# Cross-attention and mixture of experts: the first head's softmax sums on GpSimd, and an opening in another order

## The reference

```python
# cross attention: queries and keys from layernorm(x), further keys from the context
q = (ln @ Wq)                                  # per batch and head: 1024 x 64
kv = concatenate([xn @ Wkv, ln @ Wkv], axis=1)  # 77 context keys and 1024 token keys
qn, kn = rmsnorm(q, qn_g) * scale, rmsnorm(k, kn_g)
attn = softmax(einsum('bhid,bhjd->bhij', qn, kn) + mask)
x = x + einsum('bhij,bhjd->bhid', attn, v) @ Wout + bout
# then a shared expert and the best 2 of 8 experts for each token, on layernorm(x)
x = x + shared(x) + routed(x)
```

## Time and profile before

| | before |
|---|---|
| median of three runs | 2646.66 us |
| the profiled execution | 2644.76 us, span 2643.1 us |
| TensorE busy | 2502.3 us (95%) |
| VectorE busy | 1857.7 us (70%) |
| ScalarE busy | 1691.6 us (64%) |
| GpSimd busy | 1312.2 us (50%) |
| mean granted TensorE clock | 0.978 of full |

### The profile page before, as it was taken

The page is one execution under the profiler, slowest core; times in us unless marked ns, Lnnn a source line. Parts: engine busy times, 40 slices in busy tenths (PEclk is TensorE's granted clock), DMA queues, the critical chain, the costliest instruction groups (busy, mean ns, idle before and its releaser), DMA issues. The chain is left out here.

```text
span 2643.1 us, 45087 instructions
## 1 busy us (share of the span) xinstructions
PE 2502.3 (95%) x14568; PEld 2048.0 (77%) x14568; DVE 1857.7 (70%) x2507; ACT 1691.6 (64%) x2286; POOL 1312.2 (50%) x784
## 2 busy tenths in 40 slices
PE   3699999999999999999999999986989999999998
PEld 3577777777777777777777777754989999999997
DVE  6666776767777777677677767765877557776775
ACT  2477777777777777778778777774332334454453
POOL 4344553555444544454445544541542526666675
PEclk8799999999999999999999999998989999999999
DMA  5665556545664566455655565545741449999996
GB/s 186 193 159 141 155 156 165 152 134 167 165 157 133 161 162 169 131 169 151 163 148 142 162 166 149 137 131 122 169 122 55 141 145 319 321 321 321 325 320 176
DMA packets 256912, 466.62 MB, mean 177 GB/s; under 512 B 65575, under 2 KB 145755, under 8 KB 251848
## 3 DMA queue, kind: packets, MB, share of 16 engines
q1 hardware_dynamic: 230166, 406.54, 54.6%
q0 software_dynamic: 25696, 58.82, 7.9%
q10 hardware_dynamic: 978, 0.34, 0.1%
HBM read 280.90 MB, written 79.85 MB: 136 GB/s over the span
## 5 line engine op out<-in xcount | busy, mean ns | idle before, releaser
L664 DVE TENSOR_TENSOR pr_lo<-pr,pr_hi 128x1024 fp32r<-128x1024 f32 x576 | 818.5, 1429 | 356.1 <-ACT pr_hi L765 350.6
L764 ACT ACTIVATE pr<-ps_s 128x1024 f32<-128x1024 f32 x512 | 525.9, 1027 | 332.9 <-PE ps_s L883 313.5
L765 ACT ACTIVATE pr_hi<-ps_s 128x1024 fp32r<-128x1024 f32 x512 | 522.1, 1020 | 0.0
L897 PE MATMUL ps_o<-pr_hi,vA 128*65 128x512 f32 x1152 | 464.9, 404 | 20.6 <-DVE o_second L603 11.3
L410 POOL TENSOR_TENSOR sq<-raw 128x1024 f32<-128x1024 f32 (+1 forms) x96 | 183.6, 1913 | 584.6 <-ACT raw L719 584.6
L899 PE MATMUL ps_o<-pr_lo,vA 128*65 128x512 f32 x1152 | 455.1, 395 | 0.0
L898 PE MATMUL ps_o<-pr_hi,vC 128*65 128x512 f32 x1152 | 453.2, 393 | 0.0
L1547 ACT ACTIVATE ht<-f_ps_h,b 128x256 f32<-128x256 f32 x440 | 184.6, 470 | 339.7 <-PE f_ps_h L1479 339.6
L414 POOL TENSOR_TENSOR rs<-ss,minus_half 128x16 f32<-128x16 f32 (+1 forms) x96 | 261.0, 2719 | 246.0 <-DVE ss L649 246.0
L883 PE MATMUL ps_s<-qq_hi,kk 128*128 128x512 f32 x1152 | 362.8, 396 | 8.2 <-ACT pr_hi L765 6.6
L883 PE MATMUL ps_s<-qq_lo,kk 128*128 128x512 f32 x1152 | 361.7, 395 | 0.0
(11 more groups left out here) (195 smaller groups left out, 3857.0 us busy)
## 6 DMA issues: line engine op xcount, KB each, us to landing
w<-w1S_dram SPq DMA_DIRECT2D x160, 512.0 KB, 6.0
lnT_sb<-lnT_dram SPq DMA_DIRECT2D x31, 2304.0 KB, 8.5
w2raw<-in_L_ffn_Wproj SPq DMA_DIRECT2D x78, 512.0 KB, 6.9
qq_hi<-q_hi SPq DMA_DIRECT2D x128, 256.0 KB, 4.8
qq_lo<-q_lo SPq DMA_DIRECT2D x128, 256.0 KB, 5.0
kk<-k_hi SPq DMA_DIRECT2D x64, 288.0 KB, 5.1
kk<-k_lo SPq DMA_DIRECT2D x64, 288.0 KB, 5.4
w1S_dram<-cut POOLq DMA_DIRECT2D x36, 512.0 KB, 4.2
```

The costliest lines, as they stand in the source:

```text
L664: v.tensor_tensor(pr_lo[:, d % RING, :], pr[:, d % 2, :], pr_hi[:, d % RING, :].bitcast(F32), ALU.subtract).then_inc(s_lo, 1)
L764: act.activation(pr[:, d % 2, :], ps_s[:, d % 2, :], ACT.Exp, bias=bias)
L765: act.activation(pr_hi[:, d % RING, :], ps_s[:, d % 2, :], ACT.Exp, bias=bias).then_inc(s_exp, 1)
L897: mm(out, upper, pr_hi[:, r, cols], start=k == 0, stop=False)
```

## The change

**The first head (h = 0) of every window**, in the form without maxima:

- `vA` and `vC` become one tile `vv` whose 128 columns are the lower and the upper values of a head (and then two columns of ones). Per half of the queries one product of `vv` x `pr_hi` fills 128 rows of `ps_o`, with the lower values' share in rows 0 to 63 and the upper's in 64 to 127, and one product of upper values x `pr_lo` is added to rows 0 to 63. The second head keeps its three products.
- There is no row of sums then. The exponential of unit 0 goes to a new tile `total`, and GpSimd adds the `pr` of units 1 to 8 to it (`add`). ScalarE's exponentials of units 3 to 10 wait for the sum that reads the buffer they write. In unit 12 TensorE makes eight products of `total` x one column of ones (`sums`), which give the denominators on partitions; ScalarE copies them to `den`. The store, load and inversion of the row by way of DRAM goes for this head.
- At the head's end ScalarE copies rows 64 to 127 of `ps_o` to `o_sb` (`lifted`), and VectorE adds rows 0 to 63 (`output`).
- The bank of `ps_m` that a projected tile uses changes from tile 5 on (`bank_of`).
- GpSimd's third group of `normalise` moves to the next window, behind the first `add`; `lower_w` stands ahead of it now. `raw1` is half as large and loaded twice as often.

**The opening.** The weights of the second pair are loaded before the first window and split in unit 16 (before: loaded in the window, split in unit 1). The preparation of batch 1 moves to units 8 to 13 of the first opening window, that of batch 2 to units 1 to 6 and that of batch 3 to units 10 to 15 of the second; x of batch 3 and the transfers move with them.

Other lines put small tiles in places that are free at the time (`gq`, `gk`, `cstats`, `maxima`), and join semaphores. The core of the diff, in the file's order: tiles, SP queue, GpSimd, VectorE, ScalarE, TensorE.

```diff
-        vA = t.sb("vA", [P, 2, KT, 2, DH + 2], F32R)
-        vC = t.sb("vC", [P, 2, KT, 2, DH + 2], F32R)
+        vv = t.sb("vv", [P, 2, KT, 2, 2 * DH + 2], F32R)
...
+        def probabilities(d, general):
+
+            return total[:, :] if d == 0 and not general else pr[:, d % 2, :]
...
+            sp.wait_ge(s_wlo, 1)
+            load_w(1)
...
-                    spread(w, 0, 0)
-                    broadcast(w, 0, 0)
+                    if general:
+                        spread(w, 0, 0, general)
+                    broadcast(w, 0, 0, general)
...
+            def add(w, k):
+                pool.wait_ge(s_exp, w.n(UNITS, k + 1))
+                if k == 1:
+                    pool.wait_ge(s_lo, w.n(UNITS, 1))
+                else:
+                    pool.wait_ge(s_added, w.n(KT - 1, k - 1))
+                g.tensor_tensor(total[:, :], total[:, :], pr[:, k % 2, :], ALU.add).then_inc(s_added, 1)
...
+                        dve.wait_ge(s_up, w.n(2, g + 1))
+                        ins = v.tensor_tensor(o_sb[h][0:DH, half], ps_o[0:DH, g, :], o_sb[h][0:DH, half], ALU.add)
...
+            def lifted(w):
+
+                for g in range(QB):
+                    half = slice(512 * g, 512 * g + 512)
+                    if g == 0:
+                        wait(act, s_store[0], w.n(16))
+                        act.wait_ge(s_pv0, w.n(2, 1))
+                    else:
+                        act.wait_ge(s_pv, w.n(UNITS, KT))
+                    act.activation(o_sb[0][0:DH, half], ps_o[DH:2 * DH, g, :], ACT.Copy).then_inc(s_up, 1)
...
-                    if w.proj and d == (16 if w.turn else 1):
+                    if w.proj and d == 16:
...
+                        if not general and 3 <= d < KT + 2:
+                            act.wait_ge(s_added, w.n(KT - 1, d - 2))
...
-                        act.activation(pr[:, d % 2, :], ps_s[:, d % 2, :], ACT.Exp, bias=bias)
+                        act.activation(probabilities(d, general), ps_s[:, d % 2, :], ACT.Exp, bias=bias)
...
+                    if summing(w, general) and d == FIRST_PROJ + SUM_TILE:
+                        act.wait_ge(s_sum, w.n(1, 1))
+                        act.activation(den[:, 0, :], ps_m[:, SUM_TILE % 2, 0:NT], ACT.Copy).then_inc(s_summed, 1)
...
+            def sums(w):
...
+                for k in range(NT):
+                    ins = mm(ps_m[:, SUM_TILE % 2, k:k + 1], total[:, :].rearrange("p (q k) -> p k q", k=NT)[:, k, :],
+                             ones[:, 0:1].bitcast(F32), start=True, stop=True)
...
-                    mm(out, upper, pr_hi[:, r, cols], start=k == 0, stop=False)
-                    mm(out, lower, pr_hi[:, r, cols], start=False, stop=False)
-                    ins = mm(out, upper, pr_lo[:, r, cols], start=False, stop=last)
...
+                        if not last:
+                            mm(ps_o[:, q, :], vv[:, slot, k, h, 0:2 * DH], pr_hi[:, r, cols], start=k == 0, stop=False)
+                        ins = mm(ps_o[0:DH, q, :], vv[:, slot, k, h, DH:2 * DH], pr_lo[:, r, cols], start=False, stop=False)
+                        if last:
+                            ins = mm(ps_o[:, q, :], vv[:, slot, k, h, 0:2 * DH], pr_hi[:, r, cols], start=False, stop=True)
```

More of the change, by code:

```diff
@@ L78 @@
 FIRST_TURN = 2
+SUM_TILE = 5
 FIRST_PROJ = FIRST_TURN + TURNS
@@ L137, in attention @@
         nrm = t.sb("nrm", [P, KT, 4, DH])
-        gq = t.sb("gq", [P, DH])
-        gk = t.sb("gk", [P, DH])
-        gqk = t.sb("gqk", [P, DH])
+        gq, gk, gqk, gain2 = (nrm[:, 0, j, :] for j in range(4))
         k_hi = t.sb("k_hi", [P, KEYS], F32R)
@@ L182, in attention @@
         cz = rec[0:CTX, :].rearrange("p (b d) -> p b d", d=D)
-        full = raw1[:, :].rearrange("p (s n) -> p s n", s=2)
+        full = total[:, :].rearrange("p (s n) -> p s n", s=2)
         ps_s = t.ps("ps_s", [P, 2, N])
@@ L207, in attention, with summing, bank_of @@
         block = ctx.enter_context(nc.Block())
+        def probabilities(d, general):
+            return total[:, :] if d == 0 and not general else pr[:, d % 2, :]
+        def summing(w, general):
+            return w.attend and not general
+        def bank_of(w, tile, general):
+            return (tile + (summing(w, general) and tile >= SUM_TILE)) % 2
         def half_of(b, h):
@@ L309, in window @@
                     sp.wait_ge(p_out, 32)
+                if opening and w.s == 1:
+                    keep(2)
                 if w.turn:
@@ L329, in window @@
                                          src[half, :].bitcast(F32)).then_inc(s_kq[h], 16)
-                if w.proj:
+                if w.proj and not (opening and w.s == 0):
                     wait_then(s_wlo, w.n(1, 3))
@@ L341, in window @@
                 if opening and w.s == 1:
-                    for b in (2, 3):
-                        keep(b)
+                    keep(3)
                 if w.proj:
@@ L757, in window @@
                         wait(act, s_lo, w.n(UNITS, d - 1))
+                        if not general and d == 0:
+                            wait(act, s_sum, w.n(1))
+                        if not general and 3 <= d < KT + 2:
+                            act.wait_ge(s_added, w.n(KT - 1, d - 2))
                         if d % KT == KT - 1:
@@ L838, in turn, with project @@
                 ins.then_inc(s_job, 1)
-            def project(w, tile):
-                out = ps_m[:, tile % 2, :]
+            def project(w, tile, general):
+                out = ps_m[:, bank_of(w, tile, general), :]
                 if tile < 2:
```

317 lines of the change are left out of this document (185 added, 132 removed).

## The result

The changed kernel took 3155.0 us (median of 4 runs, 3154.0 to 3156.2) against 2645.7 of the kernel before (4 runs, 2644.1 to 2647.7): a ratio of 1.1925, 95% interval 1.1904 to 1.1945. It is 509 us slower. The forecast was 3010 with a range of 2870 to 3140: the direction and the main cause were right, the sum was 145 us too low, and the time lies 15 us outside the range.

A forecast was written before the change was run, and what follows sets the result against it. TensorE bounded the attention, but GpSimd's adds, excluding VectorE's subtractions, would set the first head's pace: 2644.8 + 394 (32 windows of +12.3) - 20 (opening) - 8.5 (penultimate window) = 3010 us, range 2870 to 3140.

The forecast's parts named there:

- Who may touch SBUF at once: GpSimd and VectorE: instructions with two SBUF inputs go one after the other, so each add excludes VectorE's pr_lo subtraction.
- GpSimd's queue alone: Rival, first head: adds and pr_lo subtractions overlap, so only GpSimd's own queue counts; 2670 us, chance 0.07.
- relief: Rival, TensorE: undelayed adds of 1.89 us let its removed products pay, 3.1 us a window; 2517 us, chance 0.06.
- The first head's part: Each window, end of exp(1) to start of exp(10): GpSimd's adds stretch 25.1 us to 36.65, +11.55.
- A plain unit: First head of a window: add of 2.4 plus pr_lo subtraction of 1.1 on the other engine, 3.5 us.
- split1's gap: GpSimd, first head: about 0.6 us of gap within split1, before add(7).
- the clock rival: First head: whole first part at TensorE's lower clock, its work 42 us, 5.6 above 36.6; 3190 us, chance 0.08.
- The clock falls too: Rival, first head: new TensorE gaps bring its clock to 1.2 GHz, 180 us on top of 3010; chance 0.08.
- Removed on TensorE: First head: 18 products fewer, 4.1 us a window, but TensorE then has gaps, so they give nothing.
- Opening: Before the attention windows: early weights and reordered batches end waits at w_sb and the landing; -20 us, ends -8 and -28.
- Penultimate window: Head 0's denominator no longer travels through DRAM, so TensorE's 8.53 us idle goes; -8.5 us.
- 32 second parts: Each window from exp(10) on: TensorE sets the pace, sums add 1.0, the handover counts -0.2; +0.8 us.

The follow-up runs named there:

- no_adds: The changed kernel with GpSimd's eight adds replaced by a count alone, waits and counters kept: 2781.3 us.
- no_adds_rows: The changed kernel without the GpSimd adds and with the eight sums reading neighbouring columns of total: 2674.0 us.
- opening_only: The changed kernel with the attention as before the change, keeping the new opening and GpSimd order: 2668.6 us.
- no_lo: The changed kernel with VectorE's pr_lo subtractions of units 1 to 8 cut to 8 of 1024 columns, their products reading pr_hi: 2900.9 us.
- early_weights: The kernel before, with only the second pair's weights loaded early, ahead of the first window: 2641.3 us, ratio 0.998.
- opening_rstd: opening_only with rstd of batch 2 moved ahead of the second group's rs and nrm in GpSimd's queue: 2661.0 us.
- late_lower_w: opening_rstd with GpSimd's w_sb subtraction moved back behind the third group's rs and nrm: 2637.2 us, ratio 0.997 to the kernel before.
- no_adds_split: The changed kernel without adds, its eight strided sums in two groups of four, ahead of project tile 5 and behind it: 2712.5 us.
- adds_vector: The changed kernel with the eight adds on VectorE, each right behind its unit's pr_lo subtraction, instead of on GpSimd: 2944.8 us.

## Why the prediction was right or wrong

The 509 us in four steps, each the difference of two runs:

| step | us |
|---|---|
| adds (after less no_adds) | 374 |
| stride of the sums, with the clock behind them (no_adds less no_adds_rows) | 107 |
| all else of the new attention (no_adds_rows less opening_only) | 5 |
| opening and GpSimd order (opening_only less before) | 23 |

The shares hold in this order of steps only: w_sb behind the third sq costs 24 us with the old attention and saves 14 in the changed kernel.

**Who may touch SBUF at once: right.** That add and lo exclude each other was read from two pairs in the earlier trace rows and is now shown by no_lo: adds of 2.4 beside a lo of eight columns, and 3.27 on average beside the full one (62 of the 256 took 2.4 there too). The duration of 2.4 was right to a few hundredths, and the rivals of GpSimd's queue alone and of relief are out.

**The first head's part: right within 1 us.** 36.65 forecast, 35.3 measured. Single steps were off: exp(3) waited 4.69 for add(1), which also had the cast of vv ahead of it (forecast at 6.4 after exp(1), it came at 7.5), and add(7) and add(8) began at 29.6 and not at 31.8. A plain unit took 3.3 and not 3.5, so the agreement to 1 us is in part luck: the late first add and the shorter units cancel. Two figures beside it were off in themselves: split1's gap is 0.73 in the earlier trace rows, not 0.6, and the clock rival's 42 less 36.6 is 5.4, not 5.6.

**The clock: it fell where I looked, and cost where I had not looked.** "The clock falls too" had 0.08 and 3190. The clock did fall, to 0.90 over the attention, and in the first part too. The first parts of two windows running, then their units 12, in the columns of the earlier trace rows:

```profile
1081.11:1116.52 35.41, 26.35 (x112) 19.76 (x111) 31.06 (x22) 19.26 (x26) 34.13 (x16) 0.90 0.49 138
1151.20:1186.56 35.36, 27.34 (x107) 20.67 (x106) 30.04 (x22) 19.26 (x24) 34.10 (x16) 0.81 0.49 138
1122.87:1132.56 9.69, 9.69 (x33) 8.21 (x34) 3.02 (x5) 2.60 (x4) 4.83 (x2) 0.65 0.40 99
1192.95:1201.54 8.59, 8.59 (x33) 7.30 (x34) 3.00 (x5) 2.60 (x4) 4.83 (x2) 0.80 0.43 106
```

The first part takes 35.4 us at a granted clock of 0.90 and at 0.81, since TensorE is busy only 26 to 27 of them; in unit 12, where it is busy throughout, 0.65 against 0.80 is 1.1 us. So the dear part of the fall is the one behind the one-column products, which by no_adds needs no idle time. The Trainium skill (TensorE: Matmul & The Clock Gate, Why this matters for your kernels) names idle gaps between bursts as what brings the clock down; the rows of no_adds show a fall without one.

**Removed on TensorE: its gain was nil, as forecast, but for one more reason.** Without adds and with cheap sums (no_adds_rows) a window is 0.5 us shorter than with three products (opening_only): the first part gains 1.8 and the second loses 1.3, by the sums above all. Over the attention that is 13 us, and the profiled run spent 13 more behind it, which I did not follow.

**Opening: -20 forecast, -0.6 measured.** The sum took the waits ahead of w_sb and of the landing as gone and asked only whether batches wait for their landings. It did not follow GpSimd's own order, where batch 2's rstd stood behind rs and nrm: 6 us of it come back by one moved instruction. early_weights shows the load to be worth 4.9, not 8. The rest of the 20 is not accounted for.

**GpSimd's order: +23, in no term.** I had placed w_sb "right behind" sq and counted it only into GpSimd's queue. By my own rule from the earlier trace rows I had to ask what VectorE does in those 1.8 us. Alone, w_sb's place is worth 24 (opening_rstd less late_lower_w) and batch 2's rstd 7.6; without both, the new opening is 8.3 us faster than before.

**Penultimate window: right.** TensorE's 8.53 us are gone; its longest wait from 2150 us to the attention's end is 5.6.

Taken together, against the forecast, in us:

| part | forecast | measured | difference |
|---|---|---|---|
| 32 first parts | 11.55 each | 10.6 each | -30 |
| 32 second parts, the stall of the penultimate window in them | 0.8 each, less 8.5 | 5.0 each | +143 |
| opening | -20 | -0.6 | +19 |
| last window (6 longer) and the time behind the attention (5 longer) | no term | 11 | +11 |

That is 143 of the 145.

## What to carry to other kernels

Price small products by their instructions in the trace, in the layout they will have, and ask what the clock does behind a row of them: here eight "free" column sums cost more than the eighteen wide products that they helped to remove. Where two engines exclude each other, each instruction moved on the one must be laid beside the other's timeline, the small ones too, since a 0.17 us step can hold up the whole chain. And work offered to a half-empty engine is free only if nobody waits for it in each unit.

## What the runs showed of the hardware that I had not expected

- TensorE's granted clock fell to its lower level (1.2 GHz) behind 3.7 us of one-column fp32 products with no idle time around them. Behind 1.84 us of them it did not (no_adds_rows, none of 31 windows), nor, in 20 of 31 windows, behind two groups of 1.8 to 1.9 us with six products of 384 columns between (no_adds_split).
- A weight load of 128x128 fp32 with a stride of eight elements takes 335 ns, with neighbouring columns 192.
- GpSimd's multiplication of 128x1024 fp32 by a constant takes 2.77 us, its add of two such tiles 2.35 to 2.4. The Trainium skill (GPSIMD Engine Reference, 4.1 Engine selection) has one-input work as "roughly line-rate", against a slower rate for two inputs; here the measurement decides, and the one-input multiplication is the slower of the two.
- VectorE working without a gap kept a GpSimd cast of 0.8 us from ending for 16.2 us (adds_vector).
- A GpSimd instruction with two inputs also holds a VectorE instruction of one input and two columns (opening_only, 1.44 us for 0.17). The Trainium skill (SBUF — State Buffer, Who interferes with whom) names tensor_scalar among those that can take the port that the two engines share; the trace agrees.
